# Causal attention: diagonal tiles first, their mask inside the score product and behind the exp instead of a product of its own

## The reference

```python
scores = jnp.einsum('bqhd,bkd->bhqk', q, k) * scale
bias = slopes[:, None, None] * (pos[None, None, :] - pos[None, :, None])
causal = pos[None, :] <= pos[:, None]
scores = jnp.where(causal[None, None], scores + bias[None], -jnp.inf)
attn = jax.nn.softmax(scores, axis=-1)
out = jnp.einsum('bhqk,bkd->bqhd', attn, v).reshape(b, s, h)
```

## Time and profile before

| | |
|---|---|
| median of 3 runs | 3644.59 us (3644.48 to 3645.17) |
| profiled execution | 3642.94 us, of it 3641.2 us span from the first to the last instruction |
| PE busy | 3481.5 us (96%), 20833 matmuls |
| PE weight loads busy | 2190.3 us |
| DVE busy | 2290.6 us |
| ACT busy | 1866.5 us |
| POOL busy | 1431.2 us, 435 instructions |
| granted TensorE clock, mean | 0.988 |

### The profile page before, as it was taken

The page is one execution under the profiler, slowest core; times in us unless marked ns, Lnnn a source line. Parts: engine busy times, 40 slices in busy tenths (PEclk is TensorE's granted clock), DMA queues, the critical chain, the costliest instruction groups (busy, mean ns, idle before and its releaser), DMA issues. The chain is left out here.

```text
span 3641.2 us, 56102 instructions
## 1 busy us (share of the span) xinstructions
PE 3481.5 (96%) x20833; PEld 2190.3 (60%) x20833; DVE 2290.6 (63%) x5375; ACT 1866.5 (51%) x3188; POOL 1431.2 (39%) x435
## 2 busy tenths in 40 slices
PE   5999999999999999999999999999998999999998
PEld 4555555555454554555555555454544899999997
DVE  4577777776777772677777776777762444455444
ACT  2546656665667666546656665667675101111100
POOL 1115444554657556115444554657574101011010
PEclk8999999999999999999999999999998999999999
DMA  2221110001000010221110000000012122121221
GB/s 79 55 61 30 35 48 24 25 24 42 18 19 19 19 41 19 57 62 30 36 48 24 24 24 19 19 19 18 13 58 83 47 69 65 56 69 56 65 69 41
DMA packets 158395, 148.33 MB, mean 41 GB/s; under 512 B 9396, under 2 KB 141492, under 8 KB 156056
## 3 DMA queue, kind: packets, MB, share of 16 engines
q1 hardware_dynamic: 158168, 145.34, 13.5%
HBM read 94.39 MB, written 33.62 MB: 35 GB/s over the span
## 5 line engine op out<-in xcount | busy, mean ns | idle before, releaser
L603 ACT ACTIVATE prob<-ps_s,alibi 128x512 f32<-128x512 f32 (+3 forms) x2119 | 1287.2, 633 | 741.6 <-PE ps_s L895 377.9
L540 POOL TENSOR_TENSOR prob<-prob 128x2048 f32<-128x2048 f32 (+1 forms) x240 | 1047.8, 4369 | 977.7 <-ACT prob L603 977.4
L682 DVE TENSOR_REDUCE mxp<-ps_a 128x1 f32<-128x512 f32 x1536 | 978.5, 682 | 296.0 <-PE ps_a L816 284.2
L816 PE MATMUL ps_a<-wol,qst 97*128 97x512 f32 (+3 forms) x2560 | 954.8, 395 | 37.0 <-DVE mxp L685 17.6
L895 PE MATMUL ps_s<-qst,kexp 97*128 97x512 f32 (+3 forms) x2119 | 862.7, 411 | 44.2 <-ACT prob L603 28.5
L895 PEld LDWEIGHTS ps_s<-qst,kexp 97*128 97x128 f32 x2119 | 399.0, 189 | 563.8 <-ACT prob L603 321.5
L685 DVE CUSTOM_DVE_ANT_0 ps_a<-ps_a,maska 128x128 f32<-128x128 f32 (+3 forms) x1024 | 492.4, 507 | 243.8 <-PE ps_a L816 233.3
L828 PE MATMUL ps_o<-prob,val 128*32 128x512 f32 (+3 forms) x5120 | 603.5, 543 | 9.9 <-ACT prob L603 6.6
L816 PEld LDWEIGHTS ps_a<-wol,qst 97*128 97x128 f32 x2560 | 486.5, 194 | 112.7 <-DVE mxp L685 31.9
L1089 POOL TENSOR_TENSOR work<-work,bias_b 128x1024 f32<-128x1024 f32 x32 | 76.9, 2402 | 745.4 <-DVE work L1228 710.9
L828 PE MATMUL ps_sum<-prob,ones 128*32 128x512 f32 (+2 forms) x3072 | 332.5, 505 | 3.7 <-POOL prob L540 3.3
(11 more groups left out here) (129 smaller groups left out, 3994.7 us busy)
## 6 DMA issues: line engine op xcount, KB each, us to landing
wq_raw<-in_L_attn_Wq SPq DMA_DIRECT2D x64, 512.0 KB, 3.5
work<-in_L_attn_hidden_states SPq DMA_DIRECT2D x8, 2048.0 KB, 8.3
qst<-qst SPq DMA_DIRECT2D x64, 256.0 KB
att_scratch<-at_sb SPq DMA_DIRECT2D x64, 256.0 KB, 2.8
at_raw<-att_scratch SPq DMA_DIRECT2D x32, 512.0 KB, 5.2
work<-in_L_attn_hidden_states SPq DMA_DIRECT2D x32, 512.0 KB, 4.1
out<-work SPq DMA_DIRECT2D x32, 512.0 KB, 3.1
work<-in_L_attn_Wo SPq DMA_DIRECT2D x8, 512.0 KB, 4.1
```

What stands on the lines that cost most here:

```text
L540: nc.gpsimd.tensor_tensor(even[:, :, c1:], even[:, :, c1:], odd[:, :, c1:], ALU.add).then_inc(pair_done, 1)
L603: nc.scalar.activation(prob[slot_of(steps + k)][:, h, c0:], ps_s[places[GH * (steps + k) + h][0]][:, c0:], ACT.Exp, bias=alibi_of(g, h, k ...
L682: nc.vector.tensor_reduce(top, ps, AX.X, ALU.max).then_inc(a_done, 1)
L816: last = nc.tensor.matmul(ps[:, 0:cols], qst[buf][0:KR, h, t * P:(t + 1) * P], kmax[0:KR, ring(sg):ring(sg) + cols], start=True, stop=True)
```

## The change

- Tile k of a unit is now key tile `tile_of(g, k)`: the four diagonal tiles come first (k < 4), the full ones behind them. `first_col(k)` gives the first query column.
- The mask product (line 898) is gone, and `identb` and `maskt` with it. The score of a diagonal tile uses 128 rows. Rows 97 to 127 of `kexp` say which block of 16 keys a key is in, the same rows of `qst` hold -1e30 for queries before that block. Both are built at the start by Pool (one memset and two selects of 512 elements, one memset and one select of 2048) and copied by DVE; `pool_c` is counted to 14, and four copies and the ones row stand ahead of slope4 on DVE. (A table `seen` is made as well.)
- Within the blocks the triangle is cut behind the exp: Pool's `affine_select` sets 128 columns of all four heads to 0 (MK, once per diagonal tile, signalled by `mask_done`). The PV of a diagonal tile and the ADD of a pair wait for it.
- All pairs are now summed by Pool (two more ADDs in segment 0, one more in the others), SM is gone; a quad is made in segments 2 and 3, of the four diagonal tiles.
- PV, SP, SQ and OE stand at slots of one count that runs through all units (`over_keys_at`): the PV of tile k at slot 4 (k+1) + PVD_AT (diagonal: 3, 3, 3, 1) or + PV_AT (full: 3, 3, 2, 2), so the last one falls into the next unit, OE two slots behind it; a sum goes to the slot of the first PV at or behind its own.
- The tables of slots have other values.

```diff
-        if diagonal:
-            last = nc.tensor.matmul(bank[:, c0:c0 + P], identb[:], maskt[:], start=False, stop=True)
...
+                        rows = P if k < QT else KR
+                        nc.tensor.matmul(bank[:, c0:], kexp[0:rows, at:at + P], qst[g % 3][0:rows, h, c0:],
+                                         start=True, stop=True).then_inc(s_full, 1)
...
+            def mask(g, k):
+                c0, tile = first_col(k), prob[slot_of(steps_before(g) + k)]
+                pool.wait_ge(e_done, START + GH * (steps_before(g) + k + 1))
+                nc.gpsimd.affine_select(out=tile[:, :, c0:c0 + P], in_=tile[:, :, c0:c0 + P], compare_op=ALU.is_ge,
+                                        fill=0.0, base=0, pattern=[[0, GH], [1, P]],
+                                        channel_multiplier=-1).then_inc(mask_done, 1)
...
-    return ktiles(g) // 2 - 1 if full_tiles(g) else 0
+    return ktiles(g) // 2
...
-CHUNKS_AHEAD = (7, 14, 18, 19)
-A_END = (8, 17, 31, 41)
-A_FROM = (13, 18, 31, 41)
-Q_AT = ((0, 0.5), (0, 1), (1, 1.25), (0, 1.75))
-QE_AT = ((3, 1), (7, 2), (9, 3), (12, 4))
-CT_AT = (12, 22, 35, 42)
+CHUNKS_AHEAD = (7, 14, 19, 21)
+A_END = (8, 15, 31, 42)
+A_FROM = (15, 19, 31, 42)
+Q_AT = ((1, 0.75), (0, 1), (1, 1.5), (0, 2))
+QE_AT = ((6, 1), (7, 1), (11, 3), (16, 3))
+CT_AT = (11, 22, 43, 43)
...
-THIRD = (6, 6, 2, 4)
-QUADS = (0, 0, 0, 1)
-QUAD_AT = 7
+THIRD = (4, 5, 3, 4)
+QUADS = (0, 0, 1, 1)
...
-PV_AT = (1, 1, 2, 1)
-SM_AT = (2, 1, 2, 1)
-WS_AT = (5, 21, 31, 28)
-RECIP_AT = ((0, 2, 3, 4, 11), (0, 2, 3, 5, 14), (0, 2, 5, 7, 18), (0, 2, 4, 5, 20))
+PV_AT = (3, 3, 2, 2)
+PVD_AT = (3, 3, 3, 1)
+ADD_FROM = (3, 1, 2, 3)
+OE_LAG = 2
+SUM_FROM = (0, 0, 1, 1)
+WS_AT = (12, 17, 31, 28)
+RECIP_AT = ((10, 12, 14, 15), (13, 14, 15, 20), (12, 13, 16, 18), (12, 13, 14, 17))
...
+    for t, (g, k) in enumerate(STEPS):
+        s = seg_of(g) % NSEG
+        slot = max(slot, GH * (t + 1) + (PVD_AT if k < QT else PV_AT)[s])
+        products.append(slot)
+        at.setdefault(slot, []).append(("PV", (g, k)))
+        if k == ktiles(g) - 1:
+            at.setdefault(slot + OE_LAG, []).append(("OE", g))
...
+            dve.wait_ge(pool_c, 14)
+            nc.vector.tensor_copy(kexp[3 * DH:P].rearrange("p (s c) -> p s c", c=QB),
+                                  block_of.unsqueeze(1).broadcast_to([P - 3 * DH, RING, QB])).then_inc(vec_c, 1)
+            for i in range(3):
+                nc.vector.tensor_copy(qst[i][3 * DH:P], behind[:]).then_inc(vec_c, 1)
             dve.wait_ge(vec_c, NH + 3)
+            nc.vector.memset(kexp[3 * DH:KR].bitcast(F32), 1.0).then_inc(vec_c, 1)
```

More of the change, by code:

```diff
@@ L238, in plan_unit @@
-        if k % 2 and k // 2 < summed:
-            out.append(("ADD", k // 2))
-        if k % 4 == 3 and k // 4 < quads:
-            out.append(("ADDQ", k // 4))
-    if summed:
-        out.append(("SP", summed - 1))
-    out += [("PV", n - 1), ("SM", n - 1)]
-    out.append(("OE", 0))
-    return out
+            out += OVER_KEYS.get(tiles_before(g) + i, [])
+        if k < QT:
+            out.append(("MK", (g, k)))
+        for pair in range(n // 2):
+            if k == max(2 * pair + 1, ADD_FROM[s]):
+                out.append(("ADD", (g, pair)))
+                if pair % 2 and pair // 2 < quads:
+                    out.append(("ADDQ", (g, pair // 2)))
@@ new lines, in plan_unit, with over_keys_at @@
+    if g == UNITS - 1:
+        for i in range(tiles_before(UNITS), tiles_before(UNITS) + 8 * GH):
+            out += OVER_KEYS.get(i, [])
+    return out
+STEPS = [(g, k) for g in range(UNITS) for k in range(ktiles(g))]
+def over_keys_at():
+    at, products, slot = {}, [], 0
+    for t, (g, k) in enumerate(STEPS):
[5 more added lines that the diff above has]
+            at.setdefault(slot + OE_LAG, []).append(("OE", g))
+    slot = 0
+    for g in range(UNITS):
+        s = seg_of(g) % NSEG
+        for pair in range(ktiles(g) // 2):
+            of_quad = pair < 2 * quads_summed(g)
+            if of_quad and pair % 2 == 0:
+                continue
+            step = steps_before(g) + 2 * max(pair, SUM_FROM[s]) + (5 if of_quad else 4)
+            slot = max(slot, next((x for x in products if x >= GH * step), GH * step))
+            at.setdefault(slot, []).append(("SQ", (g, pair // 2)) if of_quad else ("SP", (g, pair)))
+    return at
@@ L512, in split_wq @@
+            pool.wait_ge(pool_c, 12)
+            nc.gpsimd.memset(behind, 0.0).then_inc(pool_c, 1)
+            pool.wait_ge(pool_c, 13)
+            nc.gpsimd.affine_select(out=behind, in_=behind, compare_op=ALU.is_ge, fill=MASKED, base=0,
+                                    pattern=[[0, GH], [1, QB]], channel_multiplier=-BLOCK).then_inc(pool_c, 1)
+            pool.wait_ge(pool_c, 14)
             def split_wq(number):
@@ L910, in step @@
+                    if what in ("SP", "SQ") and arg[1] == 0:
+                        pe.wait_ge(sum_turned, START + arg[0])
                     if what == "SP":
[L911 to L912 removed]
+                        gp, pair = arg
+                        pe.wait_ge(pair_done, START + adds_until(gp, 2 * pair + 1))
+                        over_keys(gp, ps_sum, ones[:], 2 * pair, 2).then_inc(sm_done, 2)
```

132 lines of the change are left out of this document (71 added, 61 removed).

## The result

The changed kernel is slower: 3680.15 us in the median of 4 runs (3677.94 to 3683.52) beside 3644.88 for the kernel before, a ratio of 1.0094 with an interval of 1.0077 to 1.0112. The forecast was 3482, so 198 us are missing.

The account below looks back on a forecast made before the run. TensorE's instruction stream was taken as the bound. Unit savings of 3.6, 3.3, 3.1 and 1.2 us, times 16, made 179 us; 3642.9 - 179 + 17, plus 1.6 for the median, gave 3482 us, range 3420 to 3550.

Parts of the forecast that it names:

- What bounds the kernel: All attention units: TensorE's instruction stream is the limit, busy 3481.5 of 3641.2 us; distances between starts count.
- The mask matmuls, 0.12 us each, 123 us: Diagonal tiles: removing 16 mask products per unit saves 1.9 us each unit, 123 us in all.
- Rival (a): Diagonal tiles: masks are worth less, 0.08 us each, giving 41 us less gain, 3523 us; 17 in 100.
- 128 rows for 97: Diagonal scores: using 128 array rows instead of 97 was priced at zero.
- Fewer sums: Sum products per unit: 0.92, 0.25 and 0.71 us less in segments 0 to 2, 0.17 more in segment 3.
- Sums beside values, 0.66 us in segments 0 and 1: Joining sum products to value products saves 0.22 us per separate set, three per unit, in segments 0 and 1.
- Last products in the next unit, 0.5 us: Unit ends: TensorE no longer waits for the last exp, gaining 0.5 us per unit, bounds 0 to 1.2.
- Selects on Pool: Four 0.8 us selects per unit; first value product waits behind Pool's add, losing 1.0 us per segment-3 unit, elsewhere free.
- Rival (c): All segments: Pool's order binds, TensorE stands about 1 us more per unit, 64 us more, 3546 us; 11 in 100.
- ScalarE's bound in segment 0, 17.2 us: Segment 0: ScalarE's narrow half keeps a unit from going much below 17.2 us, so 0.4 of gain is lost.
- Start and end, 12 and 5: Extra tables and copies at the start lose 12 us; the last pair's add and sum product lose 5.

Follow-up runs that it names:

- experiment 5: Changed kernel with the turning and inverting of the sums placed behind the shift on VectorE in segment 0; 3669.4 us, 1.0049 of the kernel before.
- experiment 1: Kernel before, mask product replaced by 128-row diagonal scores, old order, no selects, triangle inside blocks left unmasked; 3605.4 us, 0.9873 of the kernel before.
- experiment 11: Kernel before with only segment 0's sum products moved into the slot of the value products; 3650.2 us, 1.0006 of the kernel before.
- experiment 3: Changed kernel without Pool's selects, triangle inside blocks left unmasked; 3675.8 us, 1.0068 of the kernel before.
- experiment 4: Kernel before with the complete new masking (128 rows and Pool selects) in the old order and slots; 3798.0 us, 1.0412 of the kernel before.
- experiment 7: Changed kernel with segment 1's key and value projection at slot 24 instead of 23; 3674.3 us, 1.0070 of the kernel before.
- experiment 13: Kernel before's order, mask and slots in short segments, changed kernel's in long ones, VectorE table copies off the critical start; 3619.5 us, 0.9922 of the kernel before.
- experiment 8: Changed kernel with three segment-0 table entries (query projection, its copies, start of maximum products) as before; 3748.3 us, 1.0276 of the kernel before.
- experiment 6: Changed kernel with scores of segment 0's third and fourth tile issued three times, same result; 3674.4 us, 1.0077 of the kernel before.
- experiment 2: Changed kernel with the mask product back behind each diagonal score and no selects, new order and slots kept; 3754.6 us, 1.0282 of the kernel before.

## Why the prediction was wrong, point by point

Two steps carry the miss. The mask was priced at 0.12 us at every place. And in the short segments TensorE's removed work was taken off sixteen times a middle unit, with nothing for the query chain, which now runs later, and nothing for the units beside a change of segment. Of the 167 us missing there, 105 are in the 12 units beside a change (forecast -41, measured +63), the rest in the 20 others (forecast -69, measured -6).

- **What bounds the kernel**: right as a description of before, and for the long segments after. Wrong as a ground to subtract from in segments 0 and 1: 19.52 of 20.8 us busy was read as no room for others. With TensorE's work down to 18.1 the query chain with its two transfers ends last in segment 0 (experiment 5), and the unit stays. The prediction said of the transfers only that they keep their order. In segment 1 the middle unit has 1.5 us without TensorE work (31.37 of 32.86), in waits for exps and for VectorE's maximum; which table sets that is open.
- **The mask matmuls, 0.12 us each, 123 us**: too high. 0.056 to 0.075 in the old order (0.9 x 48 + 1.2 x 16 = 62 us), 0.077 on average in the new one (79 us), where it runs from nothing in segment 0 to 0.11 in segment 2. The step that failed is "narrow scores give less cover with or without the mask, so I take 0.12 for all": the runs have 0.13 beside wide products and 0.03 to 0.06 at the others (experiment 1). Rival (a), at 0.08, had the size. The Trainium skill's figure ("TensorE: Matmul & The Clock Gate", Back-to-back issue gap, 81 ns) lies nearer to these runs than my row did.
- **128 rows for 97**: free, as taken.
- **Fewer sums**: not measured by itself. In segment 2 the middle unit of after is 0.9 us under that of experiment 1 with its mask gone as well, where this term and the end together had 1.2; in segment 3 it is 0.3 above, where they had 0.3 below, without the handoff. The difference is open.
- **Sums beside values, 0.66 us in segments 0 and 1**: wrong twice. Segment 1 had them there already, which the earlier trace rows, cut from segment 3, couldn't show and the tables could (PV_AT and SM_AT are both 1); and in segment 0 it is worth nothing (experiment 11).
- **Last products in the next unit, 0.5 us**: the wait did go, but I priced what leaves and not what stays. In before a segment-0 unit ends with value and sum products between narrow scores. In after TensorE stands 0.45, 0.73, 0.24 and 1.24 us there, and the clock falls for 3.4 us.
- **Selects on Pool**: 0.8 us taken, 0.635 measured, and the 1.0 us lost per segment-3 unit is 0 (experiment 3: 59.3 with and without selects). In the order of before they would have cost 3.0 us per unit (experiment 4). Rival (c), 64 us more because Pool's order binds, falls with experiment 3.
- **ScalarE's bound in segment 0, 17.2 us**: too low, and of the wrong engine. Its two parts, 9.5 and 7.9, add up to 17.4 besides. Durations of one engine were summed; the unit goes by the query chain of experiment 5, which takes 20.2 us at full clock.
- **Start and end, 12 and 5**: 10.0 and 5.5. Near, in part by luck: slope4 came at 22.86 where the prediction had 22.3, but the copies of 2560 and of three times 2048 columns took 2.81 and 3.49 us for the 1.9 and 4.5 taken, and these two misses cancel.
- **What wasn't in the sum at all**: the 12 units that carry or meet the work of the next segment (5 to 8, 13, 15, and their twins of the second sequence), 63 us over before together. I took a middle unit times 16. These units carry keys, values and the maximum products of a longer unit, and by the view of windows TensorE is busy 42.28 of 44.86 us in one of them before and 45 of 54 after. Part of it is shown: Pool's hold on VectorE, 3.2 us in units 13 and 45 (experiment 7); the late turn of the sums, 3 to 4 in units 5 and 37 (experiment 5). The lower clock goes with the rest; how much of it is cause and how much follows from other pauses is open. In unit 8, 5.0 us longer than before, TensorE waits for 1.9 us in all and runs 17.6 us at 1.2 GHz.

By segments, forecast and measured against before, both sequences: segment 0 -58 and +20, segment 1 -53 and +37, segment 2 -50 and -26, segment 3 -19 and -9, start and end +17 and +15.5. 167 of the 198 us are in the two short segments, and experiment 13 shows that the new order with its slots and tables loses them: with all of that taken back in the short segments the kernel is 0.8% faster than before. Which share is the order's and which the tables' isn't shown; experiment 8 put only three entries back.

## What to carry to other kernels

Subtract removed work from a unit only as far as the next chain allows, and find that chain before, transfers included: here a unit with 6% of slack on the bounding engine met it at once. When an earlier edit of such a chain changes nothing, look at when its transfer lands and not only at when it is sent. A middle unit doesn't stand for those that carry the work of a change of phase; cut one of each kind out of the trace and ask there for narrow products beside dense work of another engine. An order may be right for long units and wrong for short ones of one kernel; here the mixed kernel was the fastest, and the only one faster than before with the full computation.

## What the runs showed of the hardware that I had not expected

- A VectorE copy of one row of 512 elements within SBUF took 4.02 us while a Pool add of 4.52 ran, 1.2 under a Pool instruction of 2.34 (units 5 and 37 of after), and 0.42 otherwise (in before always). The Trainium skill states this ("SBUF — State Buffer", Who interferes with whom): VectorE's two-port copies and Pool share a pair of ports, and whoever comes second waits for the whole instruction of the other. The trace agrees, and one slot removed it. The prediction counted Pool's new work by Pool's time alone.
- Pauses of 0.2 to 1.2 us among narrow products are followed by 3.4 us and more at 1.2 GHz, in units of 20.8 us in which TensorE was busy for 18.1; 16 products more in the pauses brought the clock back to 1.00 (experiment 6), and so did the 16 mask products (experiment 2).
- A bf16 product of 128 columns between fp32 ones costs 0.13 us from start to start where wide ones stand around it, and 0.03 to 0.06 beside narrow ones or ahead of a set of value products (experiment 1).
- The shift's transfer, sent 0.56 us behind the repeat of the query, took 2.5 us to land; sent 1.3 us behind it, 1.8. Both times it landed 3.1 us after the repeat was sent, so sending it earlier gained nothing (experiment 5).
